# Causal attention on one core: query projections one step earlier, k transposes at the end of their step, the loop over groups written out

## What is computed

```python
x = _layernorm(x)                       # resid of the block is this normed x
h = _rmsnorm(x, ln1_w)
q = (h @ Wq).reshape(B, S, 32, 128)     # 32 heads, B = 4, S = 256, width 256
k = (h @ Wk).reshape(B, S, 4, 128)      # 4 groups of 8 heads share k and v
v = (h @ Wv).reshape(B, S, 4, 128)
q, k = _rope(q), _rope(k)
scores = einsum('bhqd,bhkd->bhqk', q, repeat(k, 8)) / sqrt(128)   # causal mask
o = einsum('bhqk,bkhd->bqhd', softmax(scores), repeat(v, 8)) @ Wo
x = resid + o                           # then 32 experts, top 8, and a shared one
```

## Time and profile before

| | us |
|---|---|
| median of 3 runs | 1167.24 (1165.66 to 1169.96) |
| the profiled execution | 1166.56 |
| its span, first to last instruction | 1164.8 |
| PE busy | 1042.5 (89%) |
| DVE busy | 809.1 (69%) |
| ACT busy | 693.8 (60%) |
| POOL busy | 639.1 (55%) |

### The profile page before, as it was taken

One profiled execution on the slowest core, in us unless ns is written; L12 is line 12 of the kernel. 1 busy time (PEld: TensorE's weight loads), 2 busy tenths in 40 slices (PEclk: granted clock), 3 DMA queues, 4 the chain that ended last, 5 costly groups with the idle time before them and its releaser, 6 DMA issues. The chain is left out here.

```text
span 1164.8 us, 22450 instructions
## 1 busy us (share of the span) xinstructions
PE 1042.5 (89%) x6931; PEld 914.2 (78%) x6931; DVE 809.1 (69%) x1860; ACT 693.8 (60%) x1963; POOL 639.1 (55%) x688
## 2 busy tenths in 40 slices
PE   3798987895999679998999899999979999999998
PEld 3577876784555379888998899899968888888887
DVE  6666675627888868887788788888875555555555
ACT  3455643325899568787887788777843334333342
POOL 5234312441778557775767587666633555555553
PEclk9889989897899779999999999999988999999999
DMA  8000000002213020110011000000011111111111
GB/s 250 1 1 1 2 18 16 1 1 75 89 77 133 13 82 2 47 38 4 2 47 38 4 1 2 2 1 1 2 30 42 41 54 41 54 41 46 49 41 50
DMA packets 44100, 41.78 MB, mean 36 GB/s; under 512 B 6160, under 2 KB 40048, under 8 KB 44000
## 3 DMA queue, kind: packets, MB, share of 16 engines
q1 hardware_dynamic: 42384, 39.54, 11.0%
q10 hardware_dynamic: 1616, 0.99, 0.3%
HBM read 39.40 MB, written 1.11 MB: 35 GB/s over the span
## 5 line engine op out<-in xcount | busy, mean ns | idle before, releaser
L1804 POOL TENSOR_TENSOR prob<-prob,rden 128x128 f32<-128x128 f32 (+1 forms) x256 | 124.8, 509 | 80.4 <-DVE rden L1878 80.3
L2163 POOL TENSOR_TENSOR hid_l<-hid,hid_h 128x512 fp32r<-128x512 f32 x66 | 85.6, 1297 | 134.2 <-ACT hid_h L2132 134.2
L2190 DVE TENSOR_TENSOR hid<-psum,silu 128x512 f32<-128x512 f32 x66 | 45.6, 692 | 125.5 <-ACT silu L2130 125.5
L2130 ACT ACTIVATE silu<-psum 128x512 f32<-128x512 f32 x66 | 39.4, 598 | 117.2 <-PE psum L75 117.2
L2182 DVE SCALAR_TENSOR_TENSOR x<-psum,weight,x 128x256 f32<-128x256 f32 x264 | 108.9, 475 | 0.0
L1753 ACT ACTIVATE prob<-psum,neg_max 128x128 f32<-128x128 f32 (+1 forms) x256 | 105.1, 421 | 5.3 <-issue 3.1
L73 PE MATMUL psum<-xt_h,gu_l 128*128 128x512 f32 x264 | 106.7, 404 | 0.3 <-DVE xt_l L161 0.3
L75 PE MATMUL psum<-xt_h,gu_h 128*128 128x512 f32 x264 | 105.2, 398 | 0.0
L74 PE MATMUL psum<-xt_l,gu_h 128*128 128x512 f32 x264 | 104.8, 397 | 0.0
L1294 POOL TENSOR_TENSOR drive<-u,b_all 128x1024 f32<-128x1024 f32 x32 | 75.4, 2359 | 42.5 <-DVE h L1410 20.7
L1787 POOL TENSOR_TENSOR qr<-r_part_a,r_part_b 128x512 f32<-128x512 f32 x64 | 82.9, 1295 | 8.5 <-DVE r_part_b L1838 8.5
(11 more groups left out here) (281 smaller groups left out, 3728.7 us busy)
## 6 DMA issues: line engine op xcount, KB each, us to landing
b_all<-scan_b_rows SPq DMA_DIRECT2D x16, 512.0 KB, 3.8
early<-in_L_ffn_Wq_dram SPq DMA_DIRECT2D x4, 1024.0 KB, 5.5
early<-in_L_ffn_Wo_dram SPq DMA_DIRECT2D x4, 1024.0 KB, 5.8
raw<-in_L_ffn_Wg_dram SPq DMA_DIRECT2D x32, 128.0 KB, 2.2
raw<-in_L_ffn_Wu_dram SPq DMA_DIRECT2D x32, 128.0 KB, 2.3
raw<-in_L_ffn_Wd_dram SPq DMA_DIRECT2D x32, 128.0 KB, 2.3
x<-_attn_hidden_states_dram SPq DMA_DIRECT2D x8, 128.0 KB, 4.5
early<-in_L_ffn_w_up_q_dram SPq DMA_DIRECT2D x1, 1024.0 KB, 7.1
```

The lines of the kernel that those rows point to most:

```text
L1804: ins = pool.tensor_tensor(at, at, rden[:, s % 4, i:i + 1].to_broadcast([P, (i + 1) * P]), ALU.mult)
L2163: pool.tensor_tensor(hid_l[:, j, cols], hid[:, c, :], f(hid_h[:, j, cols]), ALU.subtract)\
```

## The change

- The units' phases come one step earlier (`r - 2 * j`), and the split is divided: `split_q` (ACT) stays at phase 5, `low_q` (POOL) comes at phase 6 as the first piece of the step.
- `sum_k` (POOL's kr) is an early piece of the step r = 5, `turn_k` is the last but the weights there, `low_v` (DVE's v_l) is a piece of its own at r = 5, and the transposes wait for it through a new semaphore. The split of k (`split_k`) comes at r = 6.
- The query pieces in `WHEN` come one step earlier, at even steps.
- The three groups of the loop are written out in Python; semaphore values are constants.
- `FIRST` is new: the first queries ahead of k and v, one more query projection. `BETWEEN` spreads the z tiles (two at a time), the second half of the norm, and the output weights of the first group over steps 0 to 3.
- In the norm here, statistics and rounds of the two halves alternate (`moments`, `variance`, `rounds` = 0, 2, 1, 3); in all norms the first aggregation waits for all four statistics.

```diff
@@ -106,13 +106,19 @@
 
     def stats(self, dve, x, h, arrived=None):
 
-        own, ts = self.count, slice(h * TH, (h + 1) * TH)
         if arrived is not None:
             dve.wait_ge(*arrived[h])
+        self.moments(dve, x, h)
+        self.variance(dve, h)
+
+    def moments(self, dve, x, h):
         for t in range(h * TH, (h + 1) * TH):
-            own.add(dve.bn_stats(self.st[:, t, :], x[:, t, :]))
+            self.count.add(dve.bn_stats(self.st[:, t, :], x[:, t, :]))
+
+    def variance(self, dve, h):
+        own, ts = self.count, slice(h * TH, (h + 1) * TH)
+        own.settle()
         for t in range(h * TH, (h + 1) * TH):
-            dve.wait_ge(self.own, own.n - TH + 1)
             own.add(dve.bn_aggr(self.mv[:, t, :], self.st[:, t, :]))
         own.settle()
...
@@ -1599,7 +1606,7 @@
         PIECE = 512
         KV, Q, O = [("kv", 0)], [("q", n) for n in range(2 * KD)], [("o", n) for n in range(REP1 // 2)]
         PIECES = len(KV + Q + O)
-        WHEN = dict(zip((6, 8, 10, 12, 14, 21, 23, 25, 27), KV + O + Q))
+        WHEN = dict(zip((6, 8, 10, 12, 14, 20, 22, 24, 26), KV + O + Q))
 
         def weight_piece(g, kind, n):
...
@@ -1622,6 +1629,15 @@
                 own = not last or n < STEPS
                 (gg, s), more = at(0), own and (not last or n // REP1 + 1 < B)
                 b, r = s // REP1, s % REP1
+                units = {}
+                for j in range(4):
+                    if own if r < 2 * j else more:
+                        to, batch = (gg, b) if r < 2 * j else ahead_b(gg, b + 1)
+                        units[(r - 2 * j) % REP1] = to, 2 * batch + j // 2, j % 2
+                if 6 in units:
+                    yield "low_q", *units[6]
+                if more and r == 5:
+                    yield "sum_k", *ahead_b(gg, b + 1)
                 if own and (not last or n + 1 < STEPS):
                     yield "scores", *at(1)
                 if own:
@@ -1630,12 +1646,8 @@
                     yield "peak", *at(1)
                 if n >= 2 and (not last or n < STEPS + 2):
                     yield "turn_probs", *at(-2)
-                units = {}
-                for j in range(4):
-                    phase = (r - (2 * j + 1)) % REP1
-                    if own if r < 2 * j + 1 else more:
-                        to, batch = (gg, b) if r < 2 * j + 1 else ahead_b(gg, b + 1)
-                        units[phase] = to, 2 * batch + j // 2, j % 2
+                if more and r == 6:
+                    yield "split_k", *ahead_b(gg, b + 1)
                 if 5 in units:
                     yield "split_q", *units[5]
                 for phase in (2, 3):
@@ -1648,7 +1660,7 @@
                 if more and r == 4:
                     yield "rotate_k", *ahead_b(gg, b + 1)
                 if more and r == 5:
-                    yield "turn_k", *ahead_b(gg, b + 1)
+                    yield "low_v", *ahead_b(gg, b + 1)
                 if n >= 3 and (not last or n < STEPS + 3):
                     yield "values", *at(-3)
                 if n >= 4:
@@ -1658,14 +1670,19 @@
                 for phase in (1, 0):
                     if phase in units:
                         yield "q", *units[phase], phase
+                if more and r == 5:
+                    yield "turn_k", *ahead_b(gg, b + 1)
                 if not last and s in WHEN:
                     yield "weights", gg + 1, *WHEN[s]
 
-        FIRST = [("kv", 0, 0, 0), ("kv", 0, 0, 1), ("q", 0, 0, 0, 0), ("q", 0, 0, 0, 1), ("copy_v", 0, 0), ("rotate_k", 0, 0),
-                 ("rotate", 0, 0, 0, 0), ("rotate", 0, 0, 0, 1), ("add", 0, 0, 0), ("q", 0, 0, 1, 0), ("q", 0, 0, 1, 1),
-                 ("turn_k", 0, 0), ("split_q", 0, 0, 0), ("norm_rest",), ("scores", 0, 0), ("peak", 0, 0),
-                 ("rotate", 0, 0, 1, 0), ("rotate", 0, 0, 1, 1), ("add", 0, 0, 1), ("q", 0, 1, 0, 0), ("q", 0, 1, 0, 1),
-                 ("rotate", 0, 1, 0, 0), ("q", 0, 1, 1, 0)]
+        FIRST = [("q", 0, 0, 0, 0), ("q", 0, 0, 0, 1), ("kv", 0, 0, 0), ("kv", 0, 0, 1), ("rotate", 0, 0, 0, 0),
+                 ("rotate", 0, 0, 0, 1), ("copy_v", 0, 0), ("rotate_k", 0, 0), ("low_v", 0, 0), ("add", 0, 0, 0),
+                 ("sum_k", 0, 0), ("q", 0, 0, 1, 0), ("q", 0, 0, 1, 1), ("turn_k", 0, 0), ("split_q", 0, 0, 0), ("low_q", 0, 0, 0),
+                 ("split_k", 0, 0), ("scores", 0, 0), ("rotate", 0, 0, 1, 0), ("rotate", 0, 0, 1, 1), ("peak", 0, 0),
+                 ("add", 0, 0, 1), ("q", 0, 1, 0, 0), ("q", 0, 1, 0, 1), ("split_q", 0, 0, 1), ("normalise_rest",),
+                 ("rotate", 0, 1, 0, 0), ("rotate", 0, 1, 0, 1), ("q", 0, 1, 1, 0), ("q", 0, 1, 1, 1)]
+        BETWEEN = {0: [("z", 0), ("wo_low", 0), ("turn_rest",), ("wo_low", 1)], 1: [("z", 2), ("low_rest",), ("wo_low", 2)],
+                   2: [("z", 4), ("wo_low", 3)], 3: [("z", 6)]}
 
         def run(eng, does):
 
@@ -1675,8 +1692,11 @@
                     if kind in does:
                         does[kind](*what)
 
-            all_of([*FIRST, *schedule(0, 0, 4, False)])
-            with eng.Fori(0, KVH1 - 1) as g:
+            all_of(FIRST)
+            for n in range(4):
+                all_of(schedule(0, n, n + 1, False))
+                all_of(BETWEEN[n])
+            for g in range(KVH1 - 1):
...
+                def turn_rest():
                     norm.scalar(act, (1,))
+
+                def residual(first):
                     act.wait_ge(shifted, 1)
-                    for t in range(NT):
+                    for t in (first, first + 1):
...
+                for piece in Q:
                     weights(0, *piece)
+
+                def wo_low(n):
+                    weights(0, *O[n])
 
...
-                run(pool, dict(add=add, split_q=split_q, rotate_k=rotate_k, softmax=softmax, weights=weights))
+                run(pool, dict(add=add, low_q=low_q, sum_k=sum_k, wo_low=wo_low, softmax=softmax, weights=weights))
 
             @block.vector
             def _(dve):
                 norm.begin(dve)
-                for h in range(2):
-                    norm.stats(dve, core.x, h)
-                for h in range(2):
-                    norm.again(dve, h)
-                dve.scalar_tensor_tensor(shift[:], norm.mv[:, :, 0], -1.0, norm.rs[:], ALU.mult, ALU.mult).then_inc(shifted, 1)
+                norm.moments(dve, core.x, 0)
+                norm.variance(dve, 0)
+                norm.moments(dve, core.x, 1)
...
@@ -1837,21 +1866,24 @@
                     else:
                         dve.tensor_tensor(b, b, sin, ALU.mult).then_inc(q_parts, 1)
 
+                def low_v(g, b):
+                    bank = psum[:, KVB, :].rearrange("p (t n) -> p t n", t=2)
+                    dve.tensor_tensor(v_l[:, b % 2, :], bank[:, 0, HD1:], f(v_h[:, b % 2, :]), ALU.subtract)\
+                        .then_inc(v_lo, 1)
+
                 def rotate_k(g, b):
                     index = k_order(g, b)
                     dve.wait_ge(v_hi, index + 1)
                     if not known(index, 1):
                         dve.wait_ge(k_roped, index)
-                    bank = psum[:, KVB, :].rearrange("p (t n) -> p t n", t=2)
-                    dve.tensor_tensor(v_l[:, b % 2, :], bank[:, 0, HD1:], f(v_h[:, b % 2, :]), ALU.subtract)
-                    src = bank[:, :, 0:HD1]
+                    src = psum[:, KVB, :].rearrange("p (t n) -> p t n", t=2)[:, :, 0:HD1]
                     dve.tensor_tensor(k_part_a[:], src, tables[:, 0, :, :], ALU.mult)
                     for c in range(2):
                         lo, hi = slice(c * HD1 // 2, (c + 1) * HD1 // 2), slice((1 - c) * HD1 // 2, (2 - c) * HD1 // 2)
                         ins = dve.tensor_tensor(k_part_b[:, :, lo], src[:, :, hi], tables[:, 1, :, lo], ALU.mult)
                     ins.then_inc(k_parts, 1)
 
-                def turn_k(g, b):
+                def split_k(g, b):
                     dve.wait_ge(k_hi, k_order(g, b) + 1)
                     dve.tensor_tensor(k_l[:, b % 2, :], psum[:, KVB, 0:S], f(k_h[:, b % 2, :]),
                                       ALU.subtract).then_inc(k_lo, 1)
@@ -1893,8 +1925,8 @@
...
                     pe.wait_ge(k_roped, k_order(g, b) + 1)
+                    pe.wait_ge(v_lo, k_order(g, b) + 1)
                     for i in range(2):
...
                     b = s // REP1
+                    if s == 0 and known(g, 1):
+                        norm.ready(pe, 1)
                     pe.wait_ge(p_lo, STEPS * g + (s + 2))
```

More of the change, by code:

```diff
@@ L187, in gpsimd @@
     def gpsimd(self, pool, rounds=None):
-        for n in rounds or range(2 if self.twice is None else 4):
+        for n in rounds or self.rounds:
             ts = slice(n % 2 * TH, (n % 2 + 1) * TH)
             to, src = ((self.rs, self.ve), (self.rs2, self.ve2))[n // 2]
-            pool.wait_ge(self.var_ready, self.vars_before + n + 1)
+            pool.wait_ge(self.var_ready, self.vars_before + self.rounds.index(n) + 1)
```

(10 more changed lines are left out.)

31 lines of the change are left out of this document (17 added, 14 removed).

## The result

The changed kernel took 1148.8 us (median of 6 runs, 1144.7 to 1159.5), the kernel before 1166.7 us (6 runs, 1162.9 to 1175.7): a ratio of 0.985 (95% interval 0.980 to 0.989), 17.8 us less. The forecast was 1148 us.

The account below looks back on a forecast made before the run. The prediction took the matrix engine (PE) to set the pace, busy 89% of the span, with its waits to be gained. 5.9 + 10.3 + 2.8 + 0.0 = 19.0 us off 1166.56 gave 1148 us; forecast 1142 to 1156, 8 in 10 within 1131 to 1159.

Parts of the forecast that it names:

- A: Attention periods: moving the k transposes and q_l ends old waits of 1.52 us, adds 1.1; 5.9 us gained over 14.
- PE waits about 1.1 us for v_l: At r = 5 the moved k transposes wait 1.1 us for DVE's v_l, making the period 26.25 us.
- B: Attention groups written out and weight pieces moved to even steps: 10.3 us gained, bounds 5.2 and 11.8.
- The 5.1 us for the turns: Gaps at the loop's two backward jumps, counted from start to start, which have no place in straight code.
- Instruction blocks: Reading the longer written-out code, once instead of a body three times, costs nothing.
- The rival of 1206 us: PE runs dry at each instruction block; 33 blocks cost 58 us, so the kernel is slower; chance 0.04.
- C: Beginning of the attention stage: spread work brings step 5 to 435.1 instead of 437.94, 2.8 us gained, bounds 0 and 6.
- D: The rest: 0.4 us after the last k transposes, 0.1 for a query projection, -0.5 in the norms; together 0.0 us.
- v_l in time: Rival: v_l is ready in time, so 16 x 1.1 = 17.6 us more is gained, 1131 us; chance 0.18.
- the first three rivals: v_l ready in time (1131 us, 0.18); jump gaps are data waits (1153, 0.12); spread work eats the beginning (1159, 0.10).

Follow-up runs that it names:

- a_v_low_early: The changed kernel with v_l made at r = 4 again, ahead of the k products: 1144.9 us (kernel before on the same chip 1165.7).
- a_ot_first: The changed kernel with DVE's k products behind ot_l at r = 4 instead of ahead of it: 1152.6 us (kernel before 1165.7).
- b_written: The kernel before with its three looped groups written out, nothing else: 1155.6 us (kernel before 1163.2).
- a_loop: The changed kernel with the hardware loop over three groups put back, nothing else: 1152.9 us (kernel before 1165.7).
- a_pieces_odd: The changed kernel with the four query weight pieces at odd steps again: 1158.9 us (kernel before 1163.2).
- a_k_r2_v4: The changed kernel with k and v projected at r = 0 and 1, k products at r = 2 behind ot_l, v_l at r = 4: 1139.6 us (before 1163.2).
- after_timed: The changed kernel unchanged, timed a second time: median 1153.2 us, 0.985 of the kernel before.
- k_r2_v4_timed: The kernel of a_k_r2_v4 unchanged, timed: median 1137.5 us, 0.975 of the kernel before.
- a_z_at_once: The changed kernel with all eight z tiles behind step 0 instead of two behind each of steps 0 to 3: 1161.1 us (kernel before 1171.3).

## Why the prediction was right, step by step

- **A.** 5.9 us forecast; 14 x 0.40 = 5.6 came. The period was right to 0.02 us, and so was the cause in kind: the transposes' wait for kr goes, and DVE's lateness of about 1 us comes in. The step "PE waits about 1.1 us for v_l" failed. I followed DVE's chain to v_l, but did not ask what PE consumes from it first: ot_l of r = 4 stands behind the k products, and the values of r = 5 need it 2 us before the transposes need v_l. My "PE without waits begins r = 5 at 796.27 and is through its query matmuls at 799.2" passed over that place. The waits measured are 0.71 us at the values, 0.11 at the transposes and two of 0.19 at the values of other steps: 1.2 us in all for 1.1. That the sum agrees is partly luck. At r = 5 PE lost 0.82 us, not 1.1, and the two of 0.19 were in no term. What holds is that one lateness is paid about once: with v_l out of the way PE waited longer for ot_l, and the period stayed (a_v_low_early). An order that brings in a longer product costs more (a_ot_first).
- **B.** 10.3 us forecast. 385.2 - 14 x 26.67 = 11.8 us had been above the clean period; 370.1 - 14 x 26.27 = 2.4 us still are. So 9.5 us came. The 5.1 us for the turns was right (5.3 by b_written; 7.2 in a_loop, in the other schedule). The step that failed gave the other 6.7 us to score waits in steps crowded by ACT's weight pieces, which the new steps would relieve. The premise was wrong by the code: before, ACT split q in the even steps (phase 5 is r = 6, 0, 2, 4), and the query pieces stood in odd ones. And b_written, with these pieces where they were, gains 9.7 us by the loop alone, so 4.4 us of the 6.7 were a cost of looped code in periods with weights. Whether that is the register instructions ahead of waits, which the forecast named beside, was not tried. Against the kernel before, the new steps gave nothing that can be seen (2.2 us above the clean periods there, 2.4 us here); in this schedule they save 1.3 us (a_pieces_odd). That B came near its forecast is luck in this part. I left 1.5 us where 2.4 stayed. The Trainium skill (Advanced Engine Details and Errata, Control Flow Timing) gives 51 ns for a branch and 108 ns for a compare and branch; by that the gaps at the turns would be data waits. The trace does not agree: they vanish with the loop, and a turn took 2.6 to 4.1 us.
- **Instruction blocks**, costed at nothing: right. Over the whole run the instruction queue read 46 blocks, before 52, and PE has no unexplained gap in the periods. The rival of 1206 us is out (its sum, 33 x 1.8, is 59 and not 58 us). The row of the DMA queues, whole run of the changed kernel (packets, MB, share):

```profile
q8 instruction: 46, 0.75, 0.3%
```

- **C.** 2.8 us forecast, 2.0 came. Step 5 starts at 434.25, which is 435.97 counted from the start that the stage had before, for 435.1. And 0.9 us of its own wait (1.14 us for ot_l at 436.66) falls into the first of the 14 periods, which is why they gained 14.2 and not 15.1. The next group's weights, costed at nothing, delayed nothing: the first period (26.61) is as long as the fifth and the ninth (26.58).
- **D.** 0.5 us forecast for the tail, 1.8 came. That term was mis-sized: before, two scores without a query projection ahead of them each started 0.80 us behind the output projection (842.04, 847.22), waits that the list puts down to "issue"; q_l as the first piece of a step removes both. I had looked for them only inside the periods. b_written, with the old order, keeps all of the 38.1 us.
- **The total.** 5.6 + 9.5 + 2.0 + 1.8 - 0.9 = 18.0 us for a forecast of 19.0; the errors in B, C and D partly cancel, so a total within 1 us is luck to that extent. Of the rivals, v_l in time did not happen in the changed kernel, though a_k_r2_v4 shows what lies there: 0.6 us a period. My 16 x 1.1 = 17.6 us for it was too much: even there PE keeps small gaps of 0.1 to 0.3 us ahead of the values in four steps of a period, 0.7 us in all. The chances of the forecast and the first three rivals add up to 0.90, not 0.89.

## What to carry to other kernels

When a piece of work moves and an engine's queue is traced forward to find the new wait, list every consumer of that queue in the order in which the bound engine comes to them: the first one that is late pays, and those behind it get their data in time. If an order only decides who waits, take work out of the crowded steps, and take what is needed early out from behind a piece that waits for a third engine: v_l early alone left the period as it was (26.32), the k products early alone made it longer (26.55), and both, with the k products behind ot_l, gained 7.6 us. A hardware loop around this pipeline of four engines cost 2.6 to 4.1 us a turn and about 10 us in all, so with few turns write it out. And test each term of a sum by itself: B's total was near, with the cause of its larger part wrong.

## What the runs showed of the hardware that was not expected

- A turn of the loop cost 2.6 and 2.7 us of PE's time in the schedule before and 4.1 and 3.1 us in the new one, with 0.1 to 0.9 us more in each looped period that also splits weights. Written out, the four groups cost no stall that shows in the stage, and fewer instruction blocks.
- When DVE's sine product and POOL's q_l start together, one keeps its time (0.68 or 0.74 us) and the other takes 0.5 to 0.6 us more. In after_timed, at the same place of the schedule in two groups:

```profile
610.31 0.68 DVE L1867 TENSOR_TENSOR r_part_b<-r_part_b,rope_q 128x512 f32<-128x512 f32 x1
610.33 1.25 POOL L1818 TENSOR_TENSOR q_l<-qr,q_h 128x256 fp32r<-128x256 f32 x1
...
716.21 1.30 DVE L1867 TENSOR_TENSOR r_part_b<-r_part_b,rope_q 128x512 f32<-128x512 f32 x1
716.23 0.74 POOL L1818 TENSOR_TENSOR q_l<-qr,q_h 128x256 fp32r<-128x256 f32 x1
```

  The second time DVE was the one held up: its next piece, ot_l, came 0.6 us later, PE waited 0.59 us for it at 718.00, and the period took 27.03 us for 26.42. Every period of these runs that is longer by 0.6 us without a cause in its code holds such a sine product of 1.30 to 1.32 us. Which of the two is held up was not controlled in any run.
- The time ahead of the attention stage differed by up to 15 us between runs (389.1 in k_r2_v4_timed, 404.3 in a_z_at_once) whose code is the same there, while the stage repeated within 0.8 us. The granted clock goes with it (columns: stretch, length, busy PE, PEld, DVE, ACT, POOL, clock, DMA). The changed kernel in its first run, where the stage began at 391.7 us:

```profile
100.00:200.00 100.00, 85.63 (x618) 75.73 (x616) 64.27 (x121) 48.49 (x126) 29.22 (x21) 0.91 0.03 7
```

and the same kernel in after_timed, where it began at 398.0 us:

```profile
100.00:200.00 100.00, 89.23 (x601) 77.82 (x600) 62.60 (x118) 47.52 (x123) 29.25 (x21) 0.86 0.02 6
```

  With 0.86 for 0.91 PE gets through 601 instead of 618 matmuls in that stretch. What decides it was not tried. A single time of this program is worth no more than some 7 us either way; a stage between fixed marks is worth 0.8, most of it the event above, and a clean period 0.01.
